# Bias rows turned by transposing transfers, and 304 columns scaled on GpSimd: a cross-attention and ternary feed-forward kernel

## The reference

```python
h = layernorm(x, ln1_g, ln1_b)            # 256 wide
h = bitlinear(h, w1, b1)                  # rows rounded to 8 bits, ternary weights, 1024 wide
h = gelu(h)                               # exact
h = layernorm(h, ln2_g, ln2_b)            # gain ln2_g, offset ln2_b over 1024
h = bitlinear(h, w2, b2)                  # back to 256
x = x + h
```

## Time and profile before

| | |
|---|---|
| median of 3 runs | 1022.96 us |
| the profiled execution's own time | 1031.33 us |
| its span in the profile | 1029.6 us |
| busy in the span: PE, DVE, ACT, POOL | 928.8, 919.6, 937.5, 775.6 us |
| granted clock of TensorE 600 to 620, 620 to 640, 640 to 660 us | 0.50, 0.57, 1.00 |
| share of the DMA engines busy, 760 to 820 us | 0.80 |

### The profile page before, as it was taken

The page is one execution under the profiler, slowest core; times in us unless marked ns, Lnnn a source line. Parts: engine busy times, 40 slices in busy tenths (PEclk is TensorE's granted clock), DMA queues, the critical chain, the costliest instruction groups (busy, mean ns, idle before and its releaser), DMA issues.

```text
span 1029.6 us, 26169 instructions
## 1 busy us (share of the span) xinstructions
PE 928.8 (90%) x7492; PEld 562.4 (55%) x7524; DVE 919.6 (89%) x1194; ACT 937.5 (91%) x2675; POOL 775.6 (75%) x1187
## 2 busy tenths in 40 slices
PE   9999999999999999999999868888888888888887
PEld 7666566666666666666666413334444444444435
DVE  3688788888888888888888899999999999999998
ACT  5898899998988899999997888999999999999996
POOL 2466656777666666666667686999999999999997
PEclk9999999999999999999999966999999999999999
DMA  5699987787779776776675523877887788777785
GB/s 165 146 178 178 194 152 169 168 155 158 166 153 174 160 166 164 168 164 167 160 160 126 126 61 72 121 126 122 122 122 122 122 122 122 122 122 122 122 123 94
DMA packets 271280, 145.68 MB, mean 141 GB/s; under 512 B 178776, under 2 KB 261720, under 8 KB 271216
## 3 DMA queue, kind: packets, MB, share of 16 engines
q1 hardware_dynamic: 253632, 127.98, 60.7%
q0 software_dynamic: 16320, 15.73, 13.2%
q10 hardware_dynamic: 1264, 1.18, 0.3%
HBM read 71.36 MB, written 33.63 MB: 102 GB/s over the span
## 4 chain that ended last, share of the span: by engine, by line
PE 37%; DVE 22%; issue 15%; DMA 12%; POOL 6%; ACT 5%; SPq 2%; DVEq 1%; ACTq 0%; POOLq 0%
DMA r_rows<-x_r 9%; PE banks L1447 7%; PE banks L1433 7%; DVE g_max L883 6%; DVE gn_low L871 4%; PE banks L1347 4%; PE banks L1404 4%; DVE gn_high L871 3%; PE banks L1393 3%; DMA r_bc<-r_rows 3%; PE banks L1424 2%; DVE nm_part L771 2%; POOL nq L604 2%; PE banks L1414 2%; DVE gn_high L857 2%
## 5 line engine op out<-in xcount | busy, mean ns | idle before, releaser
L1281 PE MATMUL banks<-w_t,h_t 128*128 128x512 bf16 x473 | 130.9, 399 | 81.8 <-DVE gn_low L857 39.3
L1064 ACT ACTIVATE probs<-banks 120x512 f32<-120x512 f32 x256 | 132.3, 602 | 21.8 <-PE banks L1382 19.4
L1121 ACT ACTIVATE banks<-banks,h_dq 128x1024 f32<-128x1024 f32 x128 | 141.8, 1108 | 8.2 <-PE banks L1286 6.3
L771 DVE TRANSPOSE_TENSOR_REDUCE nm_part<-banks 128x64 f16<-128x2048 f32 x64 | 147.6, 2306 | 0.8 <-PE banks L1347 0.7
L1127 ACT ACTIVATE g_dev<-banks,g_sum 128x1024 bf16<-128x1024 f32 x128 | 145.9, 1140 | 0.0
L1447 PE MATMUL banks<-wo_sb,o_t 128*128 128x256 f32 x512 | 136.8, 399 | 1.2 <-DVE xr L777 0.9
L1315 PE MATMUL banks<-w_t,g_t 128*128 128x256 bf16 x1024 | 135.0, 276 | 1.2 <-ACT g_t L1152 1.2
L1281 PEld LDWEIGHTS banks<-w_t,h_t 128*128 (+1 forms) x504 | 47.9, 99 | 137.0 <-issue 99.3
L1433 PE MATMUL banks<-xt,wq_c 128*128 128x256 f32 x512 | 121.5, 380 | 0.0
L546 POOL COPY h_dq<-h_cl 128x2 f32<-128x2 f32 (+1 forms) x64 | 12.0, 187 | 143.8 <-DVE h_qs L836 140.8
L1315 PEld LDWEIGHTS banks<-w_t,g_t 128*128 128x128 f16 x1024 | 92.1, 98 | 50.0 <-issue 39.5
(11 more groups left out here) (179 smaller groups left out, 2553.8 us busy)
## 6 DMA issues: line engine op xcount, KB each, us to landing
x_in<-in_x SPq DMA_DIRECT2D x64, 256.0 KB, 5.8
xt<-in_x_t SPq DMA_DIRECT2D x64, 256.0 KB, 5.6
xr<-in_x SPq DMA_DIRECT2D x64, 256.0 KB, 4.4
out<-xr SPq DMA_DIRECT2D x64, 256.0 KB, 7.2
out<-h POOLq DMA_DIRECT2D x60, 256.0 KB, 5.0
ctx_t<-in_ctx_t SPq DMA_DIRECT2D x64, 128.0 KB
r_bc<-r_rows SPq DMA_DIRECT2D x61, 128.0 KB, 4.2
w_raw<-in_w_t SPq DMA_DIRECT2D x8, 256.0 KB, 6.7
```

The costliest lines, as they stand in the source:

```text
L771: dve.tensor_reduce(nm_part[:, :, 0:C * RB], blocks_p, AX.X, ALU.max, negate=True, apply_transpose=True).then_inc(max_done, 1)
L1064: act.activation(probs[:, p, j, :, :], sc_p[0:KV, j, :, :], ACT.Exp, scale=SCALE).then_inc(probs_done, 1)
L1121: act.activation(u_p[t], u_p[t], ACT.Gelu, scale=h_dq[:, b, t:t + 1], accum_out=g_sum[:, p, t:t + 1]).then_inc(gelu_done, 1)
L1281: pe.matmul(u_p[t][:, cols], h_t[:, b, t * C + c, :], w1_t[:, c, cols], start=(c == 0), stop=False, skip_group_check=True)
```

## The change

The bias rows are turned by transposing transfers on SyncE's queue, straight from `bias_row` to `bias_st`, with one semaphore `bias_turned` (16 for a pair of batches) in place of `bt_ps` and `bt_done`. The matmul and the copy go. SyncE issues one for batches 0 and 1 after its step NB - 2 of the first part, for 2 and 3 behind the loads of the gains, for 4 and 5 before its loop of the second part, and then in each even step j one for j + 4 and j + 5. Beside it PART goes from 256 to 304: of the 1024 columns GpSimd multiplies 304 by the gain and VectorE 720.

```diff
-    PART = 256
+    PART = 304
...
+                def turn_bias(b, slot):
+                    after(sp, u_ps, (b - 2) * T)
+                    after(sp, bias_turned, b * 8)
+                    sp.dma_start(bias_st[:, slot:slot + 1, :], bias_row[:, bass.ds(b, 2), :, :].rearrange("p b t n -> p (b t n)"),
+                                 transpose=True).then_inc(bias_turned, 16)
+
+                def turn_first_bias():
+                    sp.wait_ge(split_chain, 5)
+                    sp.wait_ge(x_ssq, NB * T)
+                    turn_bias(0, 0)
+
+                def load_gains_turn_bias():
+                    load_gains()
+                    turn_bias(2, 1)
...
+                    if n % 2 == 0 and live(j + 4, NB):
+                        turn_bias(j + 4, n // 2)
...
+                sp.wait_ge(split_chain, 10)
+                turn_bias(4, 0)
+                steps(sp, 2, NB - 2, FFN_L0, NB - 4, ffn, 4, {FFN_L0 - 1: scales_split})
...
-                def bias_turned(b, p):
-                    act.wait_ge(bt_ps, b + 2)
-                    after(act, u_ps, (b - 2) * T)
-                    act.activation(bias_st[:, p, :], biast_p, ACT.Copy).then_inc(bt_done, 2)
...
-                        pe.wait_ge(bt_done, b + 2 - n % 2)
+                        if n % 2 == 0:
+                            pe.wait_ge(bias_turned, b * 8 + 16)
...
-                def turn_bias(b):
-                    after(pe, bt_done, b)
-                    pe.matmul(biast_p, bias_row[:, bass.ds(b, 2), :, :].rearrange("p b t n -> p (b t n)"), ident_b[:, :],
-                              start=True, stop=True).then_inc(bt_ps, 2)
...
-                    if isinstance(b, int) and b == NB - 1:
-                        pe.wait_ge(bt_done, 2)
                     pe.wait_ge(max_done, b + 1)
```

More of the change, by code:

```diff
@@ L249, in xattn_ffn @@
         split_chain = sem("split_chain")
-        bt_ps = sem("bt_ps")
-        bt_done = sem("bt_done")
+        bias_turned = sem("bias_turned")
         u_ps = sem("u_ps")
@@ L331, in xattn_ffn @@
         y2_first = [bank[0][:, 0:D], bank[1][:, 0:D]]
-        biast_p = bank[3][:, 512 - P:512]
         u_p = [pair_a.rearrange("p a n -> p (a n)"), pair_b.rearrange("p a n -> p (a n)")]
@@ L382, in load_gains @@
                         sp.dma_start(dst[:, :], src.rearrange("(a n) -> a n", a=1).to_broadcast([P, F])).then_inc(gains_loaded, 16)
-                aside = {0: load_last, 1: load_rows, W_STEP - 1: load_bias, W_STEP + 9: store_bias, W_STEP + 13: place_bias, NB - 1: load_gains}
+                def turn_bias(b, slot):
[10 more added lines that the diff above has]
+                    turn_bias(2, 1)
+                aside = {0: load_last, 1: load_rows, W_STEP - 1: load_bias, W_STEP + 9: store_bias, W_STEP + 13: place_bias,
+                         NB - 2: turn_first_bias, NB - 1: load_gains_turn_bias}
                 aside.update({W_STEP + n: (lambda n=n: load_weight(n)) for n in range(8)})
@@ L446, in ffn, with scales_split @@
                         sp.dma_start(g_t[:, b % 4, t, :, :], nq[:, p, t, :], transpose=True).then_inc(g_turned[p], 16)
-                steps(sp, 2, NB - 2, FFN_L0, NB - 4, ffn, 4)
+                    if n % 2 == 0 and live(j + 4, NB):
+                        turn_bias(j + 4, n // 2)
+                def scales_split():
+                    sp.wait_ge(split_chain, 15)
+                sp.wait_ge(split_chain, 10)
+                turn_bias(4, 0)
+                steps(sp, 2, NB - 2, FFN_L0, NB - 4, ffn, 4, {FFN_L0 - 1: scales_split})
                 def store_last(b, t, count):
@@ L1111, in attn @@
                                            bias=x_sum[:, p, t:t + 1], accum_out=x_dev[:, p, t:t + 1]).then_inc(x_ssq, 1)
-                    if isinstance(i, int) and i == NB - 1:
-                        bias_turned(0, 0)
                     if live(i, NB) and not (isinstance(i, int) and i == 0):
@@ L1169, in ffn @@
                     gelu(j, 1, p)
[L1170 to L1175, removed]
                     if live(b, NB):
@@ L1322, in rows_down @@
                         pe.wait_ge(w2_summed, 1)
-                        pe.wait_ge(bt_done, 8)
                     pe.wait_ge(g_turned[r % 2], 16 * (b - r % 2) + 32)
@@ L1333, in ffn @@
                         rows_up(j + 1, 1, (n + 1) % 4)
[L1334 to L1337, removed]
                     if live(j - 4, NB):
@@ L1468, in attn @@
                     if isinstance(i, int) and i == NB - 1:
-                        pe.wait_ge(split_chain, 5)
                         pe.wait_ge(w2_summed, 1)
-                        turn_bias(0)
                     if live(i - 2, NB):
@@ L1505, in attn @@
                         pe.wait_ge(bias_load, 16 * HC)
-                        pe.wait_ge(bt_done, 2)
+                        pe.wait_ge(bias_turned, 16)
                         pe.wait_ge(turned[0], 16)
@@ L1516, in _ @@
                 project(NB - 2, 0)
-                pe.wait_ge(split_chain, 10)
-                turn_bias(2)
                 pe.wait_ge(x1_done, NB - 1)
@@ L1528, in all_rows @@
                         pe.wait_ge(turned[r], NB * 4)
-                    pe.wait_ge(split_chain, 15)
                 steps(pe, 4, NB, FFN_L0, FFN_L1, ffn, 4, {FFN_L0 - 1: all_rows})
```

## The result

The changed kernel takes 1030.77 us (median of 5 runs, 1028.93 to 1032.18) against 1022.96 us (5 runs on the same chip): a ratio of 1.0072, with a 95% interval of 1.0054 to 1.0089. It is slower by 5.5 to 9.1 us. The forecast was +3.9 us: the sign and the mechanism came, the size is about half. Ratios are taken over executions timed in turns with the kernel before, without the three of all the runs that ran in a slower state, and so need not be the quotient of two medians.

What follows compares the result with a forecast made beforehand. VectorE was taken to bound the batch loop at 6.43 us a batch, passing to GpSimd at 6.55. Loop and end +4.7, start -0.8, gave +3.9 us: 1026.8 us, own range 1024.8 to 1029.5, whole range 1016 to 1031.

Steps and rivals of the forecast that it cites:

- The bound passes from VectorE to GpSimd: Batch loop: VectorE's pace of 6.43 us a batch gives way to GpSimd's 6.55, with L621 at 0.83 us.
- bounds put around the cost of the columns: GpSimd's L621 at 304 columns: the 48 more cost between nothing and 0.137 us, 0.101 taken.
- second rival: Batch loop: GpSimd bounds, but with some 0.05 us more spare a batch or a 1.6 ns slope; about 1024 us, 20%.
- The loop, +7.5: Batch loop: GpSimd's chain grows 11.7 us over 58 batches, less 4.2 spare; its last L632 comes 7.5 us later.
- The lead of 2.2 us: VectorE's L871 behind GpSimd's L632: 2.2 us used up in some ten batches, so VectorE's last batch comes 5.3 us later.
- L968 near 1.3 us: End of kernel: VectorE's L968 starts before GpSimd's L700 and takes some 1.3 us instead of 4.10.
- The tail, -2.8 in the sum: TensorE's last turns: of the 7.6 us delay, 2.7 of waiting and 0.2 go, so the end moves 4.7 us.
- the 0.2 us in front of the last turn: TensorE's row near the end: 0.2 us taken off the delay, beside the 2.7 us of waiting for L968.
- fourth rival: TensorE's granted clock: its rise 5 us earlier or later moves some 1.5 us, a loop fall several; over 1040, 4%.
- The start, -0.8: Start of the second part: bias-copy waits and shorter L857 gain, longer L621 and batch 4's transfer cost; -1.3 to +0.5 us.
- The transfers, 0: SyncE's new bias transfers in the loop: landing well before use, at most 4.2 us against 17, they cost 0.
- first rival: GpSimd's L621: 48 columns cost under 0.0375 us, GpSimd keeps up and VectorE's 6.33 sets the pace; 1016.7 us, 26%.

Runs made afterwards that it cites:

- 268: The changed kernel with PART = 268 in place of 304: 1027.38 us, ratio 1.0010 to the kernel before.
- 352: The changed kernel with PART = 352 in place of 304: 1047.47 us, ratio 1.0201 to the kernel before.
- part only: The kernel before with PART = 304, the bias still turned by TensorE and copied by ScalarE: 1034.66 us, ratio 1.0072.
- tail filled: The changed kernel with twelve unused 512-column matmuls on TensorE ahead of its wait near the end: 1035.37 us, ratio 1.0084.
- kernel with the wait: The changed kernel with PART = 268 and GpSimd's last additions (L721) held until VectorE's last rounding (L989) is done: 1024.45 us, ratio 0.9983.
- 256 of 304: The changed kernel with GpSimd multiplying only 256 of its 304 columns, the other 48 left without gain: 1023.21 us, ratio 0.9944.
- before again: The kernel before without any edit, run and profiled a second time: ratio 1.0002, profiled time 1024.37 us.
- turns only: The changed kernel with PART back at 256, so only the transposing bias transfers remain: 1028.08 us, ratio 1.0009.

## Why the prediction was right, and where its size was off

The median lies outside the forecast's own range (1024.8 to 1029.5) and only 0.2 us inside the whole one (1016 to 1031), whose upper end had been set for a steeper slope of L621. That slope didn't come, so that the range held is partly luck. Term by term:

- **The bound passes from VectorE to GpSimd: right, shown.** L642 takes 0.833 us (forecast 0.83), the stores stand 6.555 us apart (6.55), and taking the 48 columns off GpSimd alone turns the loss into a gain. The bounds put around the cost of the columns weren't needed: 256, 268, 304 and 352 columns give 6.35 (its own length), 6.405, 6.56 and 6.775 us a batch, 2.13 ns a column between 256 and 304, so the second rival's 1.6 ns didn't come either.
- **The loop, +7.5: right.** The last L632, from the sixth batch's, comes 380.40 - 373.17 = 7.2 us later by its start. The last one overlaps the store before it and is shown with 1.49 us instead of 1.10; by its end it is 7.6 later.
- **The lead of 2.2 us: right in its place, without its use.** VectorE runs at its own 6.34 us a batch up to 689.86, and the batch at 696.44, the tenth, is the first that comes late (forecast: some ten batches). The waits that the profile puts down to L653 begin later, at 722.65, and show in 10 batches only. VectorE's last L892 starts 1.58 us after the last L653's start, against 3.37. That is 1.8 us given back on VectorE, but VectorE no longer sets the end.
- **L968 near 1.3 us: right.** It took 0.75 or 0.76 us in the four kernels in which it was over before L721 started (after, part only, 352, tail filled), and 4.1 to 4.7 us in the five in which the two ran beside each other. There it ended about 0.6 us behind the two additions, which took 3.45 us, not much more than the 3.1 to 3.3 they took alone. The kernel with the wait changes nothing but this overlap: 4.21 against 1.11 us. On this the forecast cites a rule (the Trainium skill, SBUF — State Buffer, section "Who interferes with whom"). The trace agrees that one of the two is blocked for the whole of the other. That the first to issue wins isn't shown: L968's record opens 0.09 us before L721's in before and 0.68 us before it with GpSimd at 256 of 304, and VectorE was blocked each time; a record doesn't show which one was given the way.
- **The tail, -2.8 in the sum (4.7 instead of 7.5): this is the term that was mis-sized.** It is -1.1: from the end of the last L632 to the end of the span there were 1029.60 - 1012.13 = 17.47 us, and there are 1027.30 - 1010.89 = 16.41. TensorE's row was taken over from the profile of before with its durations at 2.4 GHz. Now a wait of 2.85 us for L625 stands in front of that row, and at half clock it is 1017.78 - 1013.20 = 4.58 us from one L1313 to the next, where before had 1017.70 - 1014.36 = 3.34 between its L1309s: 1.2 us more. Filling the wait kept the clock and gave back the same 1.2 us of the chain. The other 0.5 us were in the forecast's gain itself: the 0.2 us in front of the last turn didn't come (3.35 us from turn to turn, 3.36 in before), and in place of the 2.69 us for L968 there is now a wait of 0.33 us for ScalarE's copy to g_t (L1166). The fourth rival had looked for a fall of the clock in the loop, where none came (1.00 from 760 to 820 us), and not where a wait opens for other reasons.
- **The start, -0.8: not resolved.** The waits for the bias copy are gone (L1376 is L1373 and waits for nothing). But the start of the seven profiles with the transfers has a mean of 59.3 us (58.4 to 60.2) and of the three with the copy 60.2 (58.9 to 61.6). The difference has the forecast's size, with a scatter as large, and the scatter goes with TensorE's clock. Its rise from half to full in before and in after:

```profile
620.00:630.00 10.00, 7.83 (x22) 2.32 (x23) 9.32 (x8) 8.83 (x23) 6.93 (x9) 0.50 0.37 69
630.00:640.00 10.00, 10.00 (x40) 4.04 (x38) 8.61 (x8) 7.71 (x19) 5.75 (x11) 0.64 0.28 52
```

```profile
620.00:630.00 10.00, 9.34 (x43) 4.16 (x43) 9.28 (x11) 8.47 (x24) 7.06 (x11) 0.77 0.40 75
630.00:640.00 10.00, 8.29 (x48) 3.84 (x47) 10.00 (x8) 10.00 (x26) 9.48 (x14) 1.00 0.49 79
```

By the granted clock of each microsecond, the rise comes 54 to 55 us after the last L771 in after, 268, 352 and before again, whose starts are 58.4 to 58.9 us, and 58 to 59 us after it in before, turns only, 256 of 304, tail filled and the kernel with the wait, whose starts are 59.5 to 60.2. Each group holds kernels with the copy and with the transfers, within 0.5 us of each other; part only fits neither (57 and 61.6). So the 1.6 us by which after's start is shorter than before's goes for the most part with this rise, which the forecast's fourth rival had priced at some 1.5 us for 5, and little of the 0.8 can be the change's; no run tests it alone. The stretch at half clock is 37.5 us long in before and 34.1 in after, a change below the 5 us that the forecast had named as a sign of being wrong.

- **The transfers, 0: right.** No wait in the loop, and the one at batch 4 lay under another.

The stages give 7.6 - 1.1 and between 0 and -0.9: +5.6 to +6.5 us, and the timed runs 5.5 to 9.1. So 1.7 us of the missing 3.5 are the tail's, up to 0.8 the start's, and the rest is within what the runs can tell; that it has one cause more isn't excluded. The first rival's ground, that the unprofiled runs are 8.4 us shorter because GpSimd is faster in them, fell with the second profile of the kernel before: it was 7 us shorter with the same loop.

## What to carry to other kernels

Where three engines run within 2% of each other, take each one's chain from the distance of its repeats in a stretch without waits, and not from busy shares: GpSimd was full at 96%, and two slopes (2.1 ns a column on GpSimd, 1.0 on VectorE) gave the pace at 268 columns, where the two chains meet, as 6.40 us against 6.405 measured. A gain worked out from matmul durations holds only as long as no new wait stands in front of them, since the granted clock can fall behind it, as it did here behind 2.85 us. And compare profiles by stage from a common mark: here the first part, in which the edits touch next to nothing, differed by up to 7.4 us between executions (last L771 at 570.59 to 578.02) and turned the sign of the totals.

## What the runs showed of the hardware that was not expected

- Near the end of the kernel TensorE waited 2.85 us in after and in part only and 3.06 with 352 columns, and the granted clock fell to 0.50 each time, for about 3.4 us. Behind waits of 2.69, 2.68 and 2.75 us in before, before again and turns only it stayed at 1.00, as it did behind the waits of the loop, at most 1.0 us in after. With 2.54 us of matmuls in the place of the 2.85 it stayed at 1.00. Whether the length of the wait decided, or what TensorE did ahead of it, these rows don't tell.
- A transposing transfer of 128 by 128 elements took 1.13 us of SyncE's queue, hardly less than the 1.22 of an h_t transfer of four times its size, and 2.3 to 6.1 us to land (median 3.9), where the g_t transfers, of eight times its size, landed in 3.1 to 4.2 in before.
- VectorE's tensor-scalar from fp32 to fp16 took 0.75, 1.11 or 4.1 to 4.7 us for the same 1024 columns, by what GpSimd ran beside it. Why it was 1.11 and not 0.75 with the additions held back isn't shown.
- GpSimd's two-input instruction took 0.243, 0.733 and 0.833 us for 24, 256 and 304 columns. That is 2.1 ns a column and, by extending the line to no columns, an estimate of 0.19 us for each instruction. On the slope the Trainium skill (GPSIMD Engine Reference, section 3.1, "Elementwise — side-by-side cycle accounting") has about 2.6 cycles an element; an estimate from it with the 1.2 GHz of the same section is 2.2 ns. The trace agrees.
